# Turning four blocks by DMA and 32x32 turns instead of on the matrix engine

## The reference

```
xn = layernorm(x)
for r in range(4):                      # rounds, cur starts as xn
    logits = cur @ Wg[r] + bg[r]        # 4 experts, the top 2 weighted by softmax -> cw
    hmid = gelu(cur @ W1[e] + b1[e])    # 512 hidden units, each expert e
    cur = cur + sum_e cw[:, e] * (hmid @ W2[e] + b2[e])
out = x + mixer(xn) * silu(cur)
```

## Time and profile before

| | us |
|---|---|
| median of 3 runs (794.79 to 795.17) | 794.92 |
| the profiled execution itself | 794.79 |
| its span, first to last instruction | 793.0 |
| PE busy | 785.5 |
| DVE busy | 687.4 |
| ACT busy | 642.9 |

### The profile page before, as it was taken

The page is one execution under the profiler, slowest core; times in us unless marked ns, Lnnn a source line. Parts: engine busy times, 40 slices in busy tenths (PEclk is TensorE's granted clock), DMA queues, the critical chain, the costliest instruction groups (busy, mean ns, idle before and its releaser), DMA issues.

```text
span 793.0 us, 9961 instructions
## 1 busy us (share of the span) xinstructions
PE 785.5 (99%) x3415; PEld 623.7 (79%) x3415; DVE 687.4 (87%) x1090; ACT 642.9 (81%) x878; POOL 112.3 (14%) x135
## 2 busy tenths in 40 slices
PE   8899999999999999999999999999999999999998
PEld 7677788887888878888788887888877788888886
DVE  7979787799888789888899788987988989988998
ACT  7988888787878878888788887888777878888885
POOL 0010211111111111111011111111111111111110
PEclk9999999999999999999999999999999999999999
DMA  8434363333444425243264341653228434655453
GB/s 263 122 79 114 86 159 95 93 94 54 100 88 101 100 40 148 45 102 94 41 144 105 55 97 31 144 117 69 67 41 172 103 53 113 130 124 119 68 123 64
DMA packets 63569, 78.46 MB, mean 99 GB/s; under 512 B 36000, under 2 KB 41632, under 8 KB 59552
## 3 DMA queue, kind: packets, MB, share of 16 engines
q0 software_dynamic: 18144, 33.04, 24.7%
q1 hardware_dynamic: 45104, 44.67, 18.7%
q10 hardware_dynamic: 272, 0.13, 0.1%
HBM read 40.34 MB, written 2.36 MB: 54 GB/s over the span
## 4 chain that ended last, share of the span: by engine, by line
PE 95%; DVE 2%; ACT 1%; DMA 1%; issue 1%; POOL 0%; DVEq 0%; POOLq 0%; ACTq 0%
PE h_bank L997 15%; PE h_bank L993 15%; PE h_bank L994 15%; PE y_bank L1052 15%; PE y_bank L1053 15%; PE y_bank L1057 15%; PE p_bank L993 2%; PE p_bank L997 2%; PE p_bank L994 2%; PE r_bank L1092 1%; PE r_bank L1113 1%; DMA cw_b<-cw_scratch 0%; PE p_bank L1005 0%; DVE g_lo L693 0%; ACT g L411 0%
## 5 line engine op out<-in xcount | busy, mean ns | idle before, releaser
L411 ACT ACTIVATE g<-h_bank,b_c 128x512 f32<-128x512 f32 x512 | 329.6, 682 | 79.5 <-PE h_bank L997 78.9
L693 DVE TENSOR_TENSOR g_lo<-g,g_hi 128x1024 fp32r<-128x1024 f32 x256 | 310.1, 1222 | 83.5 <-ACT g_hi L417 81.6
L417 ACT ACTIVATE g_hi<-g 128x1024 fp32r<-128x1024 f32 x256 | 271.9, 1062 | 8.1
L359 POOL DMA_DIRECT2D cur<-tmp x126 | 111.1, 882 | 668.2 <-DVE tmp L707 539.9
L993 PE MATMUL h_bank<-cur_hi,w_hi 128*128 128x512 f32 x512 | 203.3, 397 | 0.2 <-DVE cur_hi L604 0.2
L1052 PE MATMUL y_bank<-g_hi,w_hi 128*128 128x512 f32 x508 | 201.4, 396 | 2.1 <-DVE w_lo L583 2.1
L997 PE MATMUL h_bank<-cur_lo,w_hi 128*128 128x512 f32 x512 | 203.4, 397 | 0.0
L994 PE MATMUL h_bank<-cur_hi,w_lo 128*128 128x512 f32 x512 | 202.4, 395 | 0.0
L1053 PE MATMUL y_bank<-g_hi,w_lo 128*128 128x512 f32 x508 | 201.3, 396 | 0.0
L1057 PE MATMUL y_bank<-g_lo,w_hi 128*128 128x512 f32 x508 | 139.7, 396 | 0.0
L993 PEld LDWEIGHTS h_bank<-cur_hi,w_hi 128*128 128x128 f32 x512 | 96.3, 188 | 26.8 <-issue 3.8
(11 more groups left out here) (146 smaller groups left out, 399.1 us busy)
## 6 DMA issues: line engine op xcount, KB each, us to landing
cur<-tmp POOLq DMA_DIRECT2D x126, 256.0 KB, 3.3
cw_b<-cw_scratch SPq DMA_DIRECT2D x31, 1024.0 KB, 5.1
cur<-in_x SPq DMA_DIRECT2D x8, 256.0 KB, 5.2
xn_t<-cur SPq DMA_DIRECT2D x8, 256.0 KB, 3.1
xr<-in_x SPq DMA_DIRECT2D x28, 64.0 KB, 3.4
out<-o SPq DMA_DIRECT2D x28, 64.0 KB, 2.0
cw_b<-in_w SPq DMA_DIRECT2D x4, 256.0 KB, 5.4
cw_b<-cw_scratch SPq DMA_DIRECT2D x1, 768.0 KB, 5.2
```

The costliest lines, as they stand in the source:

```text
L359: pool.dma_start(cur[:, block_of(s // E)], tmp[:, s % SUMS, :], accum_op=ALU.add).then_inc(summed, DMA)
L411: nc.scalar.activation(g[:, gb, ft * BLK:(ft + 1) * BLK], hb[ft][:, :], ACT.Gelu_apprx_tanh, bias=b1_c[:, e * FT + ft:e * FT + ft + 1]).th ...
L417: nc.scalar.activation(g_hi[:, gb, h], g[:, gb, h], ACT.Copy).then_inc(g_hi_done, 1)
L693: nc.vector.tensor_tensor(g_lo[:, gb, h], g[:, gb, h], as_f32(g_hi[:, gb, h]), ALU.subtract).then_inc(g_lo_done, 1)
```

## The change

Blocks 4 to 7 are no longer turned by PE. `stage_normed(b)` on SP stores the normalised block to a DRAM scratch of two halves, waits for it, and loads it again with four DMAs in 128 B pieces into `xr[:, b % 2]`, in the pattern of `load_x_again`. At the head of `split_cur(k)` DVE waits for the four loads and turns 32x32 blocks from `xr` into `cur`. `split_cur` of blocks 4 to 7 comes one step later, in steps 9 to 12. ACT's `scale_block` of blocks 6 and 7 waits for the store of the block two before, and `p_bank`'s counts start four lower.

```diff
+BY_PE = NB // 2
-SPLIT_AT = {2: 4, 3: 5, 4: 8, 5: 9, 6: 10, 7: 11}
+SPLIT_AT = {2: 4, 3: 5, 4: 9, 5: 10, 6: 11, 7: 12}
...
+        xn_scratch = nc.dram_tensor("xn_scratch", (2, BLK, D), f32, kind="Internal").ap()
...
             def copy_block(b):
-                sp.wait_ge(p_empty, b + 1)
+                if b < BY_PE:
+                    sp.wait_ge(p_empty, b + 1)
+                else:
+                    sp.wait_ge(cur_placed, b - BY_PE + 1)
...
+            def stage_normed(b):
+
+                q = b % 2
+                sp.wait_ge(xn_ready, b + 1)
+                sp.dma_start(xn_scratch[q].rearrange("(p t) d -> p t d", t=TPB),
+                             xn_st[:, q, :].rearrange("p (t d) -> p t d", t=TPB)).then_inc(xn_saved, DMA)
+                sp.wait_ge(xn_saved, DMA * (b - BY_PE + 1))
+                if b < BY_PE + 2:
+                    sp.wait_ge(w2_low, E)
+                else:
+                    sp.wait_ge(cur_placed, b - BY_PE - 1)
+                for c in range(D // 32):
+                    sp.dma_start(xr[c * 32:(c + 1) * 32, q, :].rearrange("p (k c) -> p k c", c=32),
+                                 turned(xn_scratch[q], c)).then_inc(xn_staged[q], DMA)
...
             copy_block(2)
             copy_block(3)
+            stage_normed(4)
             spread_gates(2)
+            stage_normed(5)
             spread_gates(3)
+            stage_normed(6)
+            stage_normed(7)
             for b in range(4, NB):
                 copy_block(b)
...
-                if b >= 2:
+                if b >= BY_PE + 2:
+                    act.wait_ge(xn_saved, DMA * (b - BY_PE - 1))
+                elif b >= 2:
                     act.wait_ge(p_full, b - 1)
...
                 elif k < NB:
-                    dve.wait_ge(p_full, k + 1)
-                    nc.vector.tensor_scalar(src, pb[:, :], 1.0, None, ALU.mult).then_inc(p_empty, 1)
-                    dve.wait_ge(p_empty, k + 1)
+                    dve.wait_ge(xn_staged[k % 2], QDMA * ((k - BY_PE) // 2 + 1))
+                    nc.vector.transpose(src, xr[:, k % 2, :]).then_inc(cur_placed, 1)
+                    dve.wait_ge(cur_placed, k - BY_PE + 1)
...
                 if first < NB:
-                    pe.wait_ge(p_empty, first + turns)
+                    pe.wait_ge(p_empty, min(first + turns, BY_PE))
+                if first == BY_PE:
+                    pe.wait_ge(cur_placed, NB - BY_PE)
...
                 for b in at_step(NORM_SCALE, s):
-                    turn_normed(b)
+                    if b < BY_PE:
+                        turn_normed(b)
```

More of the change, by code:

```diff
@@ L187, in mixer_gated_experts @@
         xn_copied = sem("xn_copied")
+        xn_saved, cur_placed = sem("xn_saved"), sem("cur_placed")
+        xn_staged = [sem(f"xn_staged{q}") for q in range(2)]
         summed = sem("summed")
@@ L222, in p_job @@
         def p_job(m, job):
-            return NB + len(JOBS) * m + job
+            return BY_PE + len(JOBS) * m + job
         def block_of(k):
             return slice(k % NB * BLK, (k % NB + 1) * BLK)
+        xn_scratch = nc.dram_tensor("xn_scratch", (2, BLK, D), f32, kind="Internal").ap()
         block = ctx.enter_context(nc.Block())
@@ L735, in parts @@
                 if turn >= 2:
-                    dve.wait_ge(p_full, NB + turn - 1)
+                    dve.wait_ge(p_full, BY_PE + turn - 1)
                 nc.vector.tensor_scalar(part_hi[:, turn % 2, :, :], src, 1.0, None, ALU.mult).then_inc(part_ready, 1)
```

## The result

The changed kernel takes 800.6 us (median of 6, 799.12 to 802.95), the kernel before 794.81 us (median of 6 beside it): ratio 1.0081, 95% interval 1.0068 to 1.0094, or 5.8 us slower. The forecast was 799.8, in a range of 794.6 to 803.8.

What follows compares the result with a forecast made beforehand. PE was taken as the bound, busy 785.5 of 793.0 us. The terms, -1.76 (turns) + 5.1 (block 6) + 1.6 (block 7) = +4.9 us, gave 799.7, or 799.8 against the median of the runs; range 794.6 to 803.8.

Steps and rivals of the forecast that it cites:

- What goes: On PE's path, four groups of four turn matmuls disappear: 4 x 0.44 = 1.76 us.
- the gelu bank: ACT's gelu frees a bank at about 84.3, PE writes it at 84.4; no stall taken, at most 0.2 us.
- g: On SP's queue, how long after a broadcast the store issued behind it lands: 0.9 us, from 0.4 to 1.6.
- none, hardly any, 5 to 7: DVE's waits before turning xr: first none, second hardly any, third 5 to 7 us for xr<-xn_scratch.
- S: Price of one 256 KB store to the DRAM scratch: 3.1 us, from 2.5 to 4.6.
- L: Price of four 64 KB loads into xr: 4.6 us, from 3.8 to 5.4.
- (C): Rival: low prices in the queue's order, turn's gain and a 1 to 3 us stall cancel; 794.6 to 796.5, chance 0.14.
- lands with them or just after: 0.1 us each: On SP's queue, the gates' 8 KB save, issued right behind four loads, adds only 0.1 us beyond them.
- 5.1 + 1.6: PE's forecast stalls: 5.1 us before g_lo of step 12 for block 6, 1.6 before logits(2) for block 7.
- The rule that loads 6 are wanted 4.15 us before the second half of `g_lo`: DVE's turn, high, low and two g_low halves take 4.15 us, so loads 6 must land by 89.6.
- (B): Rival: everything lands in time, small transfers passing beside the broadcast at low prices; 793.0, faster; chance 0.11.
- (D): Rival: each trip collides with an accumulate or a 6.3 us broadcast; +8 to +12, 803 to 807; chance 0.09.

Runs made afterwards that it cites:

- e5: Changed kernel with stores 5 and 6 issued between the gates' save and broadcast, plus logits(2) and its gates one step later; 791.80 us, ratio 0.9974.
- e7: Changed kernel without store or loads, DVE turning straight from the normalised blocks (wrong places), blocks 6 and 7 in another buffer; 792.01 us, ratio 0.9972.
- e6: Changed kernel with only blocks 6 and 7 going through DRAM, blocks 4 and 5 turned by PE; 792.58 us, ratio 0.9981.
- a2: The changed kernel run once more, unaltered, beside the kernel before; 801.23 us, ratio 1.0078.
- e1: Changed kernel with 40 idle transposes on PE ahead of the g_lo products of step 12; 798.35 us, ratio 1.0070.
- the second group: Kernels a2, e5, e6 and e7, run beside the kernel before on the same chip; median of before 794.82 us, 25 runs.

## Why the prediction was right

**What goes.** 1.76 us, shown: e5 and e7 have 1.66 on the yardstick, e6 0.87 for two turns. The 0.1 us that is missing is the gelu bank that the prediction saw nearly touch.

**What comes, and its order.** Shown. The store behind a broadcast lands after it: with the broadcasts at 71.13 and 82.84 landed after 5.2 and 6.3 us, stores 5 and 6 came 0.6 and 0.7 us behind them (g was 0.9, from 0.4 to 1.6). e4, which alters only the place of these two stores in SP's order, takes away the whole loss.

**The terms.** DVE met the four blocks without a wait, with 0.36, with 7.18 and without a wait again, as forecast (none, hardly any, 5 to 7), but for the last; in a2 it was without, 2.08 and 8.47. From the scaling of block 4 to loads 6 it was 29.5 us in the first trace, 31.7 in a2 and 28.7 in e1, whose DMAs are the same (29.1 forecast), but in the first trace the sum came out of errors that cancel, and that is luck. S was 2.6 (3.1 forecast). L was about 3.9, 4.2 and 4.1 against 4.6: on an empty queue four loads are issued in 1.9 us, as the low end had it. One came in under 4 us, which the prediction took for a sign of (C), and (C) didn't follow, because other links were longer. In their place the save of gates 3 behind loads 5, priced at 0.1 us beyond them, took 3.9 us from its own issue (SP's rows 78.93 to 82.84), where the loads ahead of it were home near 81. And the second broadcast took 6.3 us instead of 5.1. So the gates' save was a link of its own, about 1.7 us in this trace, and the step "lands with them or just after: 0.1 us each" was wrong in size here. In a2 the save took 3.9 us too, but the last of its loads came home late, at about 82.5, and the save only 0.2 us behind it. Why these DMAs were slow is not shown: an accumulate that POOL had issued at 78.21 took 4.4 us, but the save of gates 2 (69.18) went out as close behind an accumulate (68.92) and took 1.9.

**PE's stalls.** Block 6 and block 7 together: 6.3 us until the logits begin, against 5.1 + 1.6 = 6.7. The rule that loads 6 are wanted 4.15 us before the second half of `g_lo` held: the two halves ran from 95.78 to 98.1, and PE's third product followed at once, at 98.2, some 5.5 us after 92.70, where a PE that never waits would have begun it. That leaves 0.8 us for block 7, half of the 1.6. Block 7's loads were home before DVE came to them (no wait at 98.71), so its part was DVE's turn after its combine, not the DMA.

**What was not priced.** The clock. The sum had PE at full speed after its stall, where it ran at 0.50 from 96 to beyond 101 us. That is 1.06 us, all of it from the logits on, and e1 shows the same. The measured sum is -1.76 + 0.08 + 6.31 + 1.06 = 5.69 against the forecast 4.9: the stalls were 0.4 us shorter, and the clock, a term that the prediction doesn't have, was 1.06. The forecast was 0.8 us short of the median, well within its range.

**The rivals.** (B), everything in time at 793.0, falls: it needed small transfers beside the broadcast, and stores 5 and 6 landed behind it. The Trainium skill's fit, on which it leaned (DMA: Bandwidth & Descriptors, Anatomy of one DMA, fitted on GpSimd's path), gives 2.6 us for a store of 256 KB; the store on an empty queue took 2.6 us, so there the trace agrees, and 5.4 and 6.6 us behind a broadcast, which that formula for a single DMA doesn't hold. (C) fell too: it had the low prices and a stall of 1 to 3 us, and PE stood 5.5 us for block 6 alone. (D), +8 and more, is where single runs of the changed kernel come to (802.95, and 8.1 us on the yardstick of a2).

## What to carry to other kernels

Add up a new round trip over a DMA queue in the queue's order of issue, with every wait and every large transfer ahead of it, not by its bytes: here three round trips of 256 KB and two broadcasts made a chain of 29 us. A small store that something waits for belongs ahead of a broadcast, in the time in which the issuing engine waits anyway; that order alone was worth the whole loss (some 6 us). Where a stall on PE is forecast, price the lower clock behind it as well, from the point where PE and not the late engine sets the pace (here 1.06 us). And where the last consumer (here the logits) is the only one that is late, move it a step.

## What the runs showed of the hardware

- Four DMAs of 64 KB in pieces of 128 B out of DRAM, issued when SP's queue had nothing else in it, were issued in 1.9 us; each was home 1.9 to 2.8 us after its own issue, and the four together 3.9 to 4.2 us after the first, within the 2.5 to 4.6 us of single copies of 256 KB within the on-chip memory. Behind a broadcast, issuing four took 4.1 us, and each took about 7 us (e4).
- PE's clock fell to the half, 1.2 GHz, between 94 and 96 us, while PE stood (from 92.4 on, nearly without a gap before), and was full again at 102 us, after PE had begun to work again at 97.05. With 40 idle transposes in that wait it did not fall in the trace of e1. The kernel before has such a fall at about 37 us by the mean clock of 17 of 25 runs beside the second group, where PE waits 2.1 us for `w_lo`, and of 7 of 26 beside the first; those runs are 1.4 to 1.5 us longer. The traces of after, a2, e1, e4 and e7 have the same wait of 2.1 us and no fall near it. Why it falls there in some runs only was not tried.
